# Attention of a fused attention and expert kernel: maxima carried as a 49th row of the contraction, two sets of transposed stacks, rotation sums on GpSimd, and a new order of each step

## The reference

```
x = x + xattn(layernorm(x), ctx, pos, pos, Wq, Wkv, Wout, bout)
x = x + ffn(layernorm(x), ...)

xattn: q = h @ Wq; k, v = split(ctx @ Wkv)       # 32 heads of 16
       q, k = rope(q), rope(k)                   # pairs rotated by two positions
       w = softmax(q k^T / 4)                    # per batch and head, 128 x 128
       out = (w @ v) @ Wout + bout
ffn:   shared SwiGLU (inner 352) + the two best of 16 SwiGLU experts, by sigmoid scores
```

## Time and profile before

| | |
|---|---|
| median of 3 runs | 690.98 us |
| the profiled execution | 688.72 us |
| its span, first to last instruction | 686.8 us |
| TensorE matmul busy | 635.5 us (93%) |
| VectorE, ScalarE, GpSimd busy | 503.7, 368.5, 329.9 us |
| mean granted TensorE clock | 0.986 |

### The profile page before, as it was taken

How to read it: one execution, slowest core, us unless ns; L and a number is a source line. 1 busy time by engine, 2 the same in 40 slices (tenths; PEclk the granted TensorE clock), 3 DMA queues, 4 the chain that set the end, 5 groups by cost and what they waited for, 6 DMA issues and landing times.

```text
span 686.8 us, 19435 instructions
## 1 busy us (share of the span) xinstructions
PE 635.5 (93%) x7104; PEld 406.1 (59%) x7104; DVE 503.7 (73%) x976; ACT 368.5 (54%) x620; POOL 329.9 (48%) x390
## 2 busy tenths in 40 slices
PE   2779999999999999988999999999997999999992
PEld 0255666666666666656566566666664666666661
DVE  8688888888888899866485935676775676666671
ACT  4255655656566665566411115665764666666660
POOL 3434555555555555432000011467666577767562
PEclk9889999999999999999999999999999999999997
DMA  8934755344444445660322563676778855555952
GB/s 291 247 56 62 173 103 94 88 97 99 99 99 99 99 99 122 94 125 33 115 86 76 204 220 92 173 219 98 209 211 257 229 115 92 92 88 150 246 92 33
DMA packets 105296, 90.63 MB, mean 132 GB/s; under 512 B 71649, under 2 KB 75745, under 8 KB 105249
## 3 DMA queue, kind: packets, MB, share of 16 engines
q1 hardware_dynamic: 91872, 60.28, 34.2%
q0 software_dynamic: 8752, 20.71, 16.2%
q10 hardware_dynamic: 4624, 9.00, 4.0%
HBM read 69.85 MB, written 22.81 MB: 135 GB/s over the span
## 4 chain that ended last, share of the span: by engine, by line
PE 76%; DMA 7%; issue 4%; POOL 3%; ACT 3%; DVE 3%; SPq 1%; POOLq 0%; ACTq 0%; DVEq 0%
PE p_sc L725 14%; PE p_qk L694 13%; PE p_sc L694 12%; PE p_qk L505 8%; PE p_v L505 8%; PE p_pv L594 4%; DMA used_twice_too<-used_twice 3%; PE p_pv L597 3%; PE p_tr L688 2%; PE p_pv L712 2%; PE p_sc L553 2%; PE p_pv L604 2%; PE p_sc L574 2%; PE p_sc L577 1%; SPq L426 1%
## 5 line engine op out<-in xcount | busy, mean ns | idle before, releaser
L1088 DVE TENSOR_REDUCE negmax<-p_sc 128x4 f16<-128x512 f32 x128 | 79.4, 683 | 6.8 <-PE p_sc L553 5.4
L934 ACT CAST hiddenT<-p_pv 128x384 f16<-128x384 f32 x54 | 25.8, 478 | 106.0 <-PE p_pv L712 102.2
L812 ACT ACTIVATE prob<-p_sc 128x512 f32<-128x512 f32 x128 | 66.1, 604 | 20.7 <-PE p_sc L577 20.4
L1494 POOL DMA_INDIRECT out<-prob,to_at x38 | 68.2, 1796 | 10.1 <-issue 8.2
L725 PE MATMUL p_sc<-used_twice,hiddenT 128*128 128x512 f16 (+1 forms) x306 | 71.6, 379 | 0.9 <-DVE hiddenT L1218 0.9
L1474 POOL COPY from_at<-from_rows 128x1 uint32 (+1 forms) x40 | 32.3, 808 | 80.8 <-DVE from_rows L1333 77.4
L694 PE MATMUL p_qk<-used_twice,xeT 128*128 128x352 f16 x420 | 68.4, 313 | 0.6 <-DMA xeT<-xn2T_dram 0.6
L694 PE MATMUL p_sc<-used_twice,xeT 128*128 128x352 f16 x420 | 68.4, 312 | 0.0
L1214 DVE TENSOR_TENSOR hidden<-p_sc,act_g 128x352 f32<-128x352 f32 x55 | 28.8, 524 | 52.5 <-PE p_sc L694 32.1
L921 ACT COPY xeT<-p_tr 128x1024 f16<-128x1024 f16 x40 | 40.5, 1012 | 37.2 <-PE p_tr L688 35.6
L505 PE MATMUL p_qk<-used_twice,xnT 128*128 128x512 f16 x192 | 53.1, 405 | 5.3 <-DVE swp L1066 5.3
(11 more groups left out here) (180 smaller groups left out, 1482.3 us busy)
## 6 DMA issues: line engine op xcount, KB each, us to landing
w<-e SPq DMA_DIRECT2D x20, 1408.0 KB
w<-e SPq DMA_DIRECT2D x20, 512.0 KB
out<-stream SPq DMA_DIRECT2D x17, 256.0 KB, 2.0
xn_dram<-xn_parts SPq DMA_DIRECT2D x16, 256.0 KB, 2.2
xn2T_dram<-xn2T SPq DMA_DIRECT2D x16, 256.0 KB, 2.5
w<-e SPq DMA_DIRECT2D x20, 192.0 KB
xeT<-xn2T_dram ACTq DMA_DIRECT2D x14, 256.0 KB, 2.8
stream<-x ACTq DMA_DIRECT2D x1, 3072.0 KB, 16.8
```

The source lines that it names most:

```text
L812: act.activation(prob[:, c % RING, :], p_scored(c)[:], ACT.Exp, scale=SCALE).then_inc(exp_ready, 1)
L1088: dve.tensor_reduce(negmax[:, c % 2, at:at + CH], p_scored(c)[:].rearrange("p (h t) -> p h t", t=P), AX_X, ALU.max, negate=True).then_inc( ...
L1494: pool.indirect_dma_start(out=out, out_offset=bass.IndirectOffsetOnAxis(ap=to_at[:, par, u:u + 1], axis=0), in_=ye[:, par, u], in_offset=N ...
```

## The change

Line by line, the kernel after does this:

- The stack of a head has 48 rows of values and a 49th: q is high, high, low; k is high, low, high (the product of the two low parts is no longer computed). The 49th row of k is 1, that of q is 0 for `scores`. The lower half of what `q_low` and `k_low` wrote is gone: they write 128x512 instead of 128x1024. Two memsets on GpSimd set these rows at the start.
- `place_shift`, new, on ScalarE's DMA queue: two DMAs per batch copy the rows of `negmaxT` (16 rows of 128 float16 each) into the 49th row of `qT`, one for each of the two heads above each other. `shifted_scores` waits for them and has only the matmul of L574.
- `kT` and `qT` exist twice, by the parity of the batch; a transpose waits for the shifted scores of two batches before.
- `q_sum` and `k_sum` move from VectorE to GpSimd.
- The PSUM banks are divided anew: scores use banks 0, 1 for group 0 and 2, 3 for groups 1 to 3; shifted scores use 0, 1 for groups 0 to 2 and 2, 3 for group 3.
- All five step lists have a new order. The shifted scores of a batch begin late in the step in which they stood, and go on in the next one; everything behind them is a step later, and there is one step more (`B + 3`). At the end `sums_invert` and `normalise` of the last batch's second half stand behind the pipeline.

```diff
-        kT = used_twice_too[:, 4 * DIM:6 * DIM]...; qT = used_twice_too[:, 8 * DIM:10 * DIM]...
+        kT = [used_twice_too[:, (4 + 2 * n) * DIM:(6 + 2 * n) * DIM]... for n in range(2)]
+        qT = [... for words in (used_twice_too[:, 8 * DIM:10 * DIM], w2[:]...[:, KC * DIM:KC * DIM + 2 * DIM])]
...
         def p_scored(c):
-            return p_sc[c // 2 % 2 * 2 + c % 2]
+            return p_sc[(0, 2, 2, 2)[c // 2] + c % 2]
+        def p_shifted(c):
+            return p_sc[(0, 0, 0, 2)[c // 2] + c % 2]
...
             def turn_parts(b, par, to, ready, parts_ready, at, half):
+                if later(b, 2):
+                    sp.wait_ge(shifted, b * (NCH // 2) - (6 - 2 * half))
                 sp.wait_ge(parts_ready, b + 1)
-                if later(b, 1):
-                    sp.wait_ge(shifted, b * (NCH // 2) - (2 - 2 * half))
...
             def shifted_scores(b, par, cc):
...
-                        pe.matmul(p_scored(2 * cc + a)[...], kT[rows, ...], qT[rows, ...], start=True, stop=False)
-                    for a in range(2):
-                        rows, at = slice(a * STACK, (a + 1) * STACK), a * STACK + CH * cc + n
-                        mm = pe.matmul(p_scored(2 * cc + a)[...], ident16[rows, at:at + 1].broadcast_to([STACK, P]), negmaxT[rows, :], start=False, stop=True)
+                        mm = pe.matmul(p_shifted(2 * cc + a)[...], kT[par][rows, ...], qT[par][rows, ...], start=True, stop=True)
...
             def step(b, on):                      # TensorE, after
+                on(-4, shifted_scores, 1)
+                on(-3, scores, 3)
+                on(-4, weigh_values, 0)
+                on(-5, project_out, 0)            # 0, 1, 2, 3
+                on(-4, weigh_values, 1)
+                on(-4, shifted_scores, 2)         # 2, 3
+                on(-1, project_q, 0)              # 0, 1
+                on(-3, negmax_transpose)
+                on(-1, project_q, 2)
+                on(-4, spread_recip, 0)
+                on(-1, project_q, 3)
+                on(-2, scores, 0)                 # 0, 1
+                on(-4, weigh_values, 2)           # 2, 3
+                if isinstance(b, int) and b == B + 3:  gate(0, ...)
+                on(-5, xn2_transpose)
+                on(-2, project_v, 0)              # 0, 1
+                on(-3, shifted_scores, 0)
+                on(-2, scores, 2)
+                on(-5, gate_logits)
+                on(-4, spread_recip, 1)
+                if isinstance(b, int) and b == B + 3:  up(0, ...)
+                on(0, xn_transpose)
+                on(0, project_k, 0)               # 0, 1
...
+            def place_shift(b, par):
+                act.wait_ge(negT_ready, b + 1)
+                for a in range(2):
+                    act.dma_start(qT[par][a * STACK + SHIFT:a * STACK + SHIFT + 1, :, :], negmaxT[a * STACK:a * STACK + PAIRS, :]).then_inc(shift_placed, 16)
...
             def step(b, on):                      # ScalarE, after
+                on(-4, exp, 2)                    # 2, 3
+                on(-4, summed_v_copy, 0)
+                on(-4, exp, 4)                    # 4 to 7
                 if isinstance(b, int) and b == B + 2:  split_shared2()
+                on(-5, xn2_high)
+                on(-3, place_shift)
+                on(-1, k_high)
+                on(-4, summed_v_copy, 1)
+                on(-5, xn2T_copy)
                 on(0, ctx_high)
+                on(-3, exp, 0)
+                on(-5, keep_logits)
+                on(-3, exp, 1)
+                on(0, xnT_copy)
+                on(-4, attnT_high)
+                on(-2, v_copy)
+                on(-1, q_high)
...
             def step(b, on):                      # VectorE, after
                 on(-3, neg_copy)
+                on(-1, q_turn)
+                on(-2, row_max, 0)                # 0 to 3
+                on(-4, sums_invert, 1)
+                on(-2, row_max, 4)
+                on(-4, normalise, 1)
+                on(-2, row_max, 5)
+                on(0, xnT_low)
+                on(0, k_turn)
+                on(-2, row_max, 6)                # 6, 7
+                on(1, ln1_stats)
                 on(-4, residual)
                 on(-4, ln2_stats)
+                on(-3, sums_invert, 0)
+                on(1, ln1_norm)
                 on(-4, ln2_norm)
                 if isinstance(b, int) and b == B + 2:  split_shared2()
+                on(-3, normalise, 0)
...
             def step(b, on):                      # GpSimd, after
+                on(-5, rstd2_make)
+                on(-5, xn2_low)
+                on(-1, q_sum)
+                on(-1, k_low)
                 on(0, ctx_low)
                 on(-2, bias_add)
                 on(-4, attnT_low)
+                on(-1, q_low)
+                on(0, k_sum)
+                on(1, rstd1_make)
...
             def step(b, on):                      # SyncE, after
+                on(1, load_ctx)
+                on(-6, store_xn2T)
+                on(-1, turn_k_parts, 0)
                 on(-5, store_xn2)
+                on(-1, turn_q_parts, 0)
+                on(-1, turn_k_parts, 1)
+                on(-1, turn_q_parts, 1)
```

More of the change, by code:

```diff
@@ L445, in step @@
                         sp.dma_start(xeT[:, n].rearrange("p a c t -> p (a c t)"), xn2T_dram[n * P:(n + 1) * P]).then_inc(sems.xT_loaded[n], 16)
[L447 removed]
+            pipeline(step, sp, 1, B + 5, 7, (B - 8) // 2)
             sp.wait_ge(xn2_stored, B * 16 + 16)
@@ L770, in pair @@
                             place()
-            pipeline(step, pe, 0, B + 2, 6, (B - 6) // 2, ahead=[xn_transpose])
+            pipeline(step, pe, 0, B + 3, 6, (B - 6) // 2, ahead=[xn_transpose])
             for c in range(KC):
@@ L927, in gate_act @@
                 act.activation(act_g[:], p_g, ACT.Silu, scale=1 / W_SCALE).then_inc(sems.act_ready, 1)
-            pipeline(step, act, 0, B + 2, 6, (B - 6) // 2, ahead=[ctx_high, xnT_copy])
+            pipeline(step, act, 0, B + 3, 7, (B - 8) // 2, ahead=[ctx_high, xnT_copy])
             def hT_high(n):
@@ L1192, in step @@
                     dve.scalar_tensor_tensor(gate16[:, 1], gate_sb[:], W_SCALE, gate16[:, 0], ALU.mult, ALU.subtract).then_inc(gate_parts, 1)
-                on(-3, sums_invert, 0)
-                on(-1, k_sum)
-                on(-3, normalise, 0)
                 on(-4, ln2_norm)
@@ L1198, in step @@
                     split_shared2()
-                on(-2, row_max, 0)
-                on(-2, row_max, 1)
-                on(-2, row_max, 2)
-                on(-2, row_max, 3)
-                on(-3, sums_invert, 1)
-                on(-1, q_turn)
-                on(-3, normalise, 1)
-            pipeline(step, dve, 0, B + 2, 6, (B - 6) // 2, ahead=[ln1_stats, ln1_norm, xnT_low, k_turn, k_sum])
+                on(-3, normalise, 0)
+            pipeline(step, dve, 0, B + 2, 6, (B - 8) // 2, ahead=[ln1_stats, ln1_norm, xnT_low, k_turn])
             def hidden_make(n):
@@ L1231, in y_take @@
                     dve.tensor_scalar(ye[:, par, u], p_y[u][:], gate_at[:, bass.ds(q, 1)], None, ALU.mult).then_inc(sems.y_ready, 1)
+            sums_invert(B - 1, 1, 1)
+            normalise(B - 1, 1, 1)
             hidden_make(0)
```

178 lines of the change are left out of this document (75 added, 103 removed).

## The result

The kernel after takes **700.97 us** (median of 4 runs, 698.53 to 704.39) against 690.98 before (median of 4 runs, 685.52 to 692.36): the ratio taken over all runs is 1.0163, with a 95% interval of 1.0094 to 1.0233. It is slower by about 10 us, where 9.8 us less were forecast. The interval is 0.7% to either side, so the 0.2% that the prediction counted on was too fine. The profiled execution took 700.80 us (span 699.0), 12.1 more than that of before.

The account below looks back on a forecast made before the run. The batch loop was taken as bound by TensorE's list, with VectorE 1.9 us behind, and both attention ends by chains through other engines. -14.4 - 2.0 + 0 + 6.6 = -9.8 us gave 681.2 us, range 676.0 to 689.5.

Parts of the forecast that it names:

- TensorE's work: Attention, all batches: dropping the second matmuls of the shifted scores (L577) shortens TensorE's list by 14.4 us.
- The multiplication by 16: Attention: the second matmuls' cost of 0.9 us a batch counted as saved in all 16 batches, 14.4 us.
- Irregular waits: Loop and early steps: waits for DMA transposes should go, taking back 2.0 of 3.1 us of irregular loss.
- Beginning: First steps: `ctx_low` delays batch 1, but the first maxima transpose stays within 0.5 us; 0, between -3 and +3.
- End: Last steps: one more step and little to hide behind add 6.6 us, between +3 and +10.
- The two splits: Last steps: `split_shared2` delays ScalarE's operations in step 18 by 2.5 us and VectorE's `normalise` in step 19 by 2.8.
- The 49th row: Shifted scores: `place_shift` takes 2.8 us of the 4.3 available, so it is hidden with 1.5 us to spare.
- rival 4: Shifted scores: `place_shift` lands late and every step waits; with 6.0 us, +17.4 us, 708.4 us; chance 0.10.
- The port: Loop: GpSimd sums hold up VectorE at the shared SBUF port; 0.6 us lost a batch, +9.6; chance 0.07.
- rival 3: Loop: sums on GpSimd meet VectorE's SBUF work at the shared port; +9.6, 690.8 us, no change; chance 0.07.
- Rival 2: Both ends eat the gain: beginning +3, end +10, no irregular loss back; -1.4, 689.6 us; chance 0.08.

Follow-up runs that it names:

- e11: Kernel after with the second matmuls of the shifted scores put back, identity rows in place of the maxima; 704.34 us, ratio 1.0180 to the kernel before.
- e6: Kernel after with the shared experts' weights loaded in pieces at steps 4, 5, 6 and 15, not all at step 4; ratio 1.0094 to the kernel before.
- e5: Kernel after with the sums on VectorE in the first four steps and ScalarE's first weight parts behind `q_high`; 696.33 us, ratio 1.0072 to before.
- e3: Kernel after with the splits of the shared expert's weights moved in the last steps on VectorE and ScalarE; 696.92 us, ratio 1.0107 to before.
- e4: Kernel after with both rotation sums back on VectorE in every step; 700.93 us, ratio 1.0184 to the kernel before.
- e7: Kernel after with the last steps written out on TensorE, ScalarE and VectorE, `xeT` loaded two steps later; 688.91 us, ratio 0.9976 to before.
- e2: Kernel after with 49 unneeded matmuls at TensorE's waits in steps 16 to 19; 699.58 us, ratio 1.0153 to the kernel before.

## Why the prediction was wrong

Two steps failed, and e11 tells them apart, since it is the kernel after, order, sums and 49th row, with the old amount of matmuls. Its attention ends 15.9 us later than that of the kernel before, where the terms other than TensorE's work had -2.0 + 0 + 6.6 = +4.6. The removal then gives 5.8 us, where the prediction had 14.4. Of the 20 us between the forecast of -9.8 and the +10.2 of the attention, the new order with all that belongs to it is 11.3 and the removal 8.6. Each end time is that of one profile, and in the experiments above a part of the same program differs by up to some 2 us from one profile to the next.

- *TensorE's work, -14.4.* **The multiplication by 16 failed.** 0.9 us a batch was right (0.89), as was the loop's step (16.75 forecast, 16.61 measured). But TensorE's list is the bound only in eight steps, which together take 132.88 us in the kernel after and 140.02 in e11, 7.1 more. In the rest the new order has TensorE waiting, and putting the same matmuls back adds no time there that can be told from chance.
- *Irregular waits, -2.0.* The loop gave 7 x (1.06 - 0.89) = 1.2 us. The wait of the early steps stayed and grew, as the load of the shared experts' weights stands beside the transposes (e6).
- *Beginning, 0 (between -3 and +3).* **This failed too.** I had seen that `ctx_low` stands behind `q_sum` and `k_low`, priced the delay at 3 us, and still had the maxima transpose of batch 0 within 0.5 us of its old place. It came 4.0 us later (1.6 to 4.0 in the six profiles with this beginning): TensorE waited 4.04 us for `ctx_low`. Idle time up to batch 13 rose by 5.6 us. e5 took 7.4 us off up to batch 6, part of it by chance.
- *End, +6.6.* In idle time it was nearly right: +9.0, inside the +3 to +10, and +6.2 in e11, where the second matmuls fill a part of the waits. The two splits were where I had put them. **Priced at nothing was what the waits do to the clock**: 4.8 us at the end and, by subtraction, some 5 before. No term and no rival had it; the prediction treated durations as fixed.
- *Rivals.* The 49th row landed in time in the loop (no wait there; rival 4 refuted). The port did not bind: a step has 16.62 of 16.62 us busy, and no `ln1_norm` takes more than 0.55 us, where the kernel before has the one of 1.43 (rival 3 refuted). Rival 2 named the right places with too small a price: it had +13 for both ends beside the full -14.4, and on that reckoning they cost 5.6 + 9.0 + 9.9 = 24.5.

## What to carry to other kernels

Multiply a saving per step only by the steps in which that engine is the bound; here that was eight of 16. A new order for the loop needs its own lists for the first and the last steps, read again with every operation that was moved to another engine: there it can hold up, by waiting for its own input, what stands behind it. And when a step of the plan makes TensorE wait, price the matmuls behind the wait at the lower clock, not only the wait.

## What the runs showed that I had not expected

- A stretch can be shorter with more for TensorE to do: with 49 useless matmuls the end was 3.8 us shorter, with the granted clock at 1.00 in place of 0.95 and 0.85.
- The same beginning comes in two forms: first maxima transpose at 43.3 to 43.4 us with a clock of 0.92, or at 45.0 to 45.7 with 0.89, for the same program order. What decides between them is open.
- Beside a load of the shared experts' weights in one piece TensorE waits 1.64 to 2.56 us for transposes by DMA in six of seven profiles with the new order (0.31 in e11). In the 10 us behind the wait the clock has a mean of 0.83 or 0.84 in four of them (after, e3, e4, e7); in e2, e5 and e11 it stays at 1.00.
- A float32 sum of two SBUF operands took 0.69 us on VectorE alone, 1.51 to 1.63 when a GpSimd subtraction had begun just before it, and 1.26 to 1.29 on GpSimd.
